# Softmax without the shift pass: exponentials straight from PSUM with row sums, in a three-stage token pipeline on one core

## The reference

```python
tokens = einsum('bpi,hi->bph', patches, W) + b            # embedding: 2352 -> 128, times pos_embed
# A: 8 heads of 16, complex q, k, v; scores * decay mask; group norm; silu gate; w2
# B: layer norm, then softmax attention over the 97 tokens, 8 heads of 16, scale 1/4
x2 = layernorm(h1);  q, k, v = x2 @ Wq + bq, x2 @ Wk + bk, x2 @ Wv + bv
p = softmax(q @ k.T / 4);  z = (p @ v) @ Wo + bo + x2
# C: layer norm, gate = softmax(th @ gate_W), the best expert of each token,
#    out = residual + gate weight * (gelu(th @ W1[e] + b1[e]) @ W2[e] + b2[e])
```

## Time and profile before

| | us |
|---|---|
| median of three timed runs | 1430.12 (1424.32 to 1433.03) |
| profiled execution, time | 1419.48 |
| profiled execution, span of its instructions | 1417.7 |
| TensorE busy | 1348.5 (95%) |
| VectorE busy | 1010.9 (71%) |
| ScalarE busy | 722.7 (51%) |
| GpSimd busy | 408.4 (29%) |

### The profile page before, as it was taken

The page is one execution under the profiler, slowest core; times in us unless marked ns, Lnnn a source line. Parts: engine busy times, 40 slices in busy tenths (PEclk is TensorE's granted clock), DMA queues, the critical chain, the costliest instruction groups (busy, mean ns, idle before and its releaser), DMA issues.

```text
span 1417.7 us, 40337 instructions
## 1 busy us (share of the span) xinstructions
PE 1348.5 (95%) x14878; PEld 989.9 (70%) x14879; DVE 1010.9 (71%) x2331; ACT 722.7 (51%) x1630; POOL 408.4 (29%) x268
## 2 busy tenths in 40 slices
PE   6889999999999999999999999999999775999996
PEld 5556666666666666666666666666666444999996
DVE  1477777777777777777777777777778853766664
ACT  2145555555555555555555555555555543556553
POOL 0000222222222222222222222222222233656664
PEclk9999999999999999999999999999999975999999
DMA  8522332232223322323232222222320011343331
GB/s 292 215 83 72 83 84 83 84 83 83 84 84 83 84 84 84 83 83 84 83 84 83 84 84 84 83 84 83 84 83 14 14 30 37 105 125 103 103 101 48
DMA packets 94842, 124.61 MB, mean 88 GB/s; under 512 B 56587, under 2 KB 77117, under 8 KB 94176
## 3 DMA queue, kind: packets, MB, share of 16 engines
q1 hardware_dynamic: 38112, 102.47, 23.1%
q0 software_dynamic: 56576, 19.93, 6.5%
HBM read 101.27 MB, written 20.82 MB: 86 GB/s over the span
## 4 chain that ended last, share of the span: by engine, by line
PE 90%; DVE 4%; DMA 2%; issue 2%; ACT 1%; POOL 0%; SPq 0%; POOLq 0%; DVEq 0%; ACTq 0%
PE bank_emb L421 20%; PE bank_s L475 9%; PE bank_z L411 7%; PE bank_y L489 7%; PE bank_x L411 7%; PE bank_s L710 6%; PE bank_s L553 4%; PE bank_s L541 4%; PE bank_s L411 3%; PE bank_y L411 3%; PE bank_y L581 3%; PE bank_x L699 3%; PE bank_y L699 3%; PE bank_x L563 3%; PE bank_s L525 2%; PE bank_y L553 2%
## 5 line engine op out<-in xcount | busy, mean ns | idle before, releaser
L1397 POOL DMA_INDIRECT expert_rows<-row_sb,placei x128 | 275.7, 2154 | 627.7 <-DVE z L1058 575.6
L421 PE MATMUL bank_emb<-home_x 128*128 128x256 f32 (+1 forms) x1216 | 324.0, 393 | 3.5 <-DMA home_x<-in_x_main 2.5
L421 PEld LDWEIGHTS bank_emb<-home_x 128*128 128x128 f32 (+1 forms) x1216 | 221.4, 192 | 103.4 <-issue 47.4
L998 DVE TENSOR_TENSOR home_s<-bank_s,con 97x776 f32<-97x776 f32 x256 | 239.8, 958 | 25.9 <-PE bank_s L475 13.8
L1012 DVE TENSOR_REDUCE mx<-bank_s 97x8 f32<-97x776 f32 x128 | 120.3, 960 | 57.9 <-PE bank_s L541 57.8
L1409 POOL DMA_INDIRECT out_tokens<-yo,tok x104 | 123.1, 1184 | 73.6 <-issue 52.5
L475 PE MATMUL bank_s<-qm,xn 32*97 32x452 f32 x1024 | 132.6, 580 | 4.2 <-DVE home_s L1017 2.0
L1017 DVE TENSOR_TENSOR home_s<-bank_s,mx 97x776 f32<-97x776 f32 x128 | 120.6, 963 | 3.3
L853 ACT ACTIVATE home_s<-home_s 97x776 f32<-97x776 f32 x128 | 108.4, 847 | 26.4 <-DVE home_s L1017 26.4
L710 PE MATMUL bank_s<-w2e,home_s 128*128 x832 | 110.6, 276 | 0.0
L1005 DVE COPY vp<-bank_s 97x128 f32<-97x128 f32 x256 | 70.1, 285 | 54.9 <-PE bank_s L475 54.8
(11 more groups left out here) (206 smaller groups left out, 2339.8 us busy)
## 6 DMA issues: line engine op xcount, KB each, us to landing
home_x<-in_x_main SPq DMA_DIRECT2D x96, 768.0 KB, 7.2
home_x<-expert_rows SPq DMA_DIRECT2D x104, 129.0 KB
w1e<-in_exp_w SPq DMA_DIRECT2D x1, 2576.0 KB, 10.8
txt<-in_txt_t SPq DMA_DIRECT2D x32, 64.0 KB, 2.3
w2e<-in_exp_w SPq DMA_DIRECT2D x1, 2048.0 KB, 16.1
expert_rows<-row_sb,placei POOLq DMA_INDIRECT x128, 8.1
out_tokens<-yo,tok POOLq DMA_INDIRECT x104
home_x<-in_x_tail SPq DMA_DIRECT2D x32, 48.0 KB, 2.6
```

The costliest lines, as they stand in the source:

```text
L421: mm = pe.matmul(banks["emb"][:, 0:NPG], wtok[0:k, c, :], x_sb[0:k, c, :], start=(c == 0), stop=(c == KC - 1))
L998: ins = dve.tensor_tensor(sm[:, k % 2, 2 * h:2 * h + 2, :], pair(h), decay, ALU.mult)
L1397: pool.indirect_dma_start(out=rows[:, :], out_offset=bass.IndirectOffsetOnAxis(ap=placei[:, k, c:c + 1], axis=0), in_=row_sb[:, k, c, E:E ...
```

## The change

- B's scores carry the opposite sign (bq4 and the scale of B.q are negative). VectorE takes the minimum of each block (b_min), and ScalarE computes exp(minimum - score), head by head and sequence by sequence, straight from the score banks: 32 ACTIVATEs of 97x97 a group with the minimum as bias column and with the row sum as second output into `rsum`. b_shift is gone; the banks are drained by the last exponential of each pair.
- The row sums come from there. VectorE makes their reciprocals, spread over 16 columns each (97x512 in one instruction, sums_reciprocal), TensorE transposes these (four 97x128 tiles, b_sums) and ScalarE copies the result to `rden` (sums_copy). The 16 matmuls, the logarithm and the exponential are gone.
- The lists of the three engines and the banks in `USES` are new. A group's a_center moves from the pass before into its own, b_q, b_scores of the first half and part of the copies move one pass later, c_rank and the placing too; the loop starts one pass later (FIRST = -1) and the first list is made one pass later. The embedding is cut in 11 pieces a pass.
- At the start, token weights and images come in turns and first, then columns and position, then weights and constants; TensorE does the whole embedding of group 0 before the products of the weights. ScalarE copies `woc` first. The blank rows are written behind the expert weights.
- rsb and rsc share a buffer with sqb and sqc.
- The block ends without GpSimd's drain.

```diff
-    block = ctx.enter_context(nc.Block())
+    block = ctx.enter_context(nc.Block(no_gpsimd_drain=True))
...
             def b_exp(g, k, h):
-                read(act, g, f"B.scores{k}.{h}")
-                p = prob[:, k, 2 * h:2 * h + 2, :].rearrange("p g t -> p (g t)")
-                act.activation(p, p, ACT.Exp).then_inc(s_prob, 1)
+                act.wait_ge(s_mx, MAXED[g, k, h])
+                if g:
+                    act.wait_ge(s_rden, g)
+                for r in (2 * h, 2 * h + 1):
+                    for j in range(4):
+                        t = slice(j * S, (j + 1) * S)
+                        ins = act.activation(prob[:, k, r, t], bank_s[0:S, r, t], ACT.Exp, scale=-1.0,
+                                             bias=mx[:, k, r, j:j + 1], accum_out=rsum[:, 2 * k + j // 2, r, j % 2:j % 2 + 1])
+                drain(ins, f"B.scores{k}.{h}")
...
-            def b_sums(g, k):
-                ps = use(g, "B.den") if k == 0 else banks[BANK_OF["B.den"]]
...
+            def b_sums(g):
+                pe.wait_ge(s_rden, g + 1)
+                ps = use(g, "B.den")
+                for c in range(G):
+                    mm = pe.transpose(ps[:, c * S:(c + 1) * S], rexp[:, c, :], const("ident")[0:S, 0:S])
+                done(mm, "B.den")
...
+            def sums_reciprocal(g):
+                for k in range(2):
+                    for h in range(2):
+                        read(dve, g, f"B.scores{k}.{h}")
+                dve.reciprocal(rexp[:].rearrange("p c (q d) -> p (c q) d", d=DH),
+                               rsum[:].rearrange("p c r o -> p (c r o)").unsqueeze(2).to_broadcast(
+                                   [S, G * H, DH])).then_inc(s_rden, 1)
...
+                at(b_q, i - 2)
+                at(a_gate, i - 1)
+                at(b_probs_t, i - 3, 1, 1)
+                at(b_sums, i - 3)
+                at(b_values, i - 3)
+                at(b_scores, i - 2, 0, first=True)
+                at(a_mix, i - 1, 0)
+                at(a_mix, i - 1, 1)
+                at(b_mix, i - 3, 0)
+                at(b_mix, i - 3, 1)
+                at(ahead, i, 16, 18)
+                at(c_rank, i - 4)
                 at(b_wo, i - 3)
+                at(ahead, i, 18, 19)
+                at(a_scores, i - 1, 2)
+                at(b_probs_t, i - 2, 0, 1)
+                at(ahead, i + 1, 0, 2)
                 at(c_var, i - 3)
+                at(ahead, i + 1, 2, 3)
+                at(a_center, i)
+                at(a_scores, i - 1, 3)
+                at(b_probs_t, i - 2, 0, 0)
+                at(ahead, i + 1, 3, 5)
+                at(a_var, i)
                 at(a_mix, i - 1, 2)
                 at(a_mix, i - 1, 3)
+                at(b_scores, i - 2, 1)
+                at(a_yvar, i - 1)
...
```

More of the change, by code:

```diff
@@ L225, in fusion @@
         sqc = sb("sqc", [P, N])
[L226 removed]
+        rsc = sqc
         th = sb("th", [P, N])
@@ L339, in _ @@
             for k in range(4):
+                if k < 3:
+                    sp.dma_start(wtok[:, XP[k]:XP[k + 1], :], w_main[:, XP[k]:XP[k + 1], :]).then_inc(s_w[k], 16)
+                else:
+                    sp.dma_start(wtok[0:KTAIL, KC - 1, :], w_tail).then_inc(s_w[k], 16)
                 load_x(0, k)
+            sp.dma_start(col[:], columns).then_inc(s_c, 16)
+            sp.dma_start(pos[:], pos_t).then_inc(s_c, 16)
+            sp.dma_start(wts[:], weights).then_inc(s_k, 16)
+            sp.dma_start(con[:], consts).then_inc(s_k, 16)
             def load_txt(i):
@@ L358, in _ @@
             sp.dma_start(w2e[:], exp_w2).then_inc(s_ew, 16)
+            sp.wait_ge(s_blankin, 16)
+            sp.dma_start(rows[E * REG:E * REG + P, :], blank[:]).then_inc(s_blankin, 16)
             with sp.Fori(2, NG) as i:
@@ L549, in b_probs_t @@
                 ps = use(g, name)
-                pe.wait_ge(s_prob, PROB[g, k, r // 2])
+                read(pe, g, f"B.scores{k}.{r // 2}")
                 for j in range(4):
@@ L554, in b_probs_t @@
                 done(mm, name)
-            def b_sums(g, k):
-                ps = use(g, "B.den") if k == 0 else banks[BANK_OF["B.den"]]
-                for r in range(4):
-                    read(pe, g, f"B.probs_t{k}.{r}")
-                for o in range(2):
-                    for r in range(4):
-                        src = pt[:, k, r, :].rearrange("p (c o t) -> p c o t", c=2, o=2)[:, :, o, :]
-                        mm = pe.matmul(ps[32 * r:32 * r + 32, 2 * k * S:(2 * k + 2) * S],
-                                       const("den", S)[:, 32 * o:32 * o + 32], src, start=(o == 0), stop=(o == 1),
-                                       skip_group_check=True)
-                if k == 1:
-                    done(mm, "B.den")
+            def b_sums(g):
[4 more added lines that the diff above has]
+                done(mm, "B.den")
             def b_mix(g, k):
@@ L686, in _ @@
+                at(b_probs_t, i - 2, 1, 3)
+                at(ahead, i + 1, 11, 12)
+                at(b_center, i - 1)
+                at(a_scores, i, 1, first=True)
+                at(b_var, i - 1)
+                at(ahead, i + 1, 12, 15)
+                at(b_probs_t, i - 2, 1, 0)
+                at(b_probs_t, i - 2, 1, 2)
+                at(a_scores, i, 0)
+                at(b_probs_t, i - 2, 0, 2)
+                at(b_k, i - 1)
+                at(ahead, i + 1, 15, 16)
                 if i == LISTED:
@@ L754, in _ @@
             act.wait_ge(s_mm, 1)
+            act.copy(woc[:], banks["s2"][:, 0:P]).then_inc(s_made, 1)
             act.copy(ar[:], banks["s0"][:, 0:P])
@@ L761, in _ @@
                              banks["s1"][r32, 0:2 * P].rearrange("p (m w) -> p m w", m=2)[:, :, r32])
-            act.copy(woc[:], banks["s2"][:, 0:P]).then_inc(s_made, 1)
             act.wait_ge(s_mm, 2)
@@ L842, in b_query @@
                 ps = full(act, g, "B.q")
-                drain(act.activation(q2[:], ps[:, 0:N], ACT.Identity, bias=bq4[:], scale=0.25), "B.q")
+                drain(act.activation(q2[:], ps[:, 0:N], ACT.Identity, bias=bq4[:], scale=-0.25), "B.q")
             def b_value_rows(g):
@@ L858, in b_probs_copy, with sums_copy @@
                 drain(act.copy(pt[:, k, r, :], ps[0:S, 0:4 * S]), name)
-            def sums_log(g):
+            def sums_copy(g):
                 ps = full(act, g, "B.den")
-                drain(act.activation(rden[:], ps[:, 0:N], ACT.Ln), "B.den")
-            def sums_reciprocal(g):
-                read(act, g, "B.den")
-                act.activation(rden[:], rden[:], ACT.Exp, scale=-1.0).then_inc(s_rden, 1)
+                drain(act.copy(rden[:], ps[:, 0:N]), "B.den")
             def free_rows(g):
@@ L1049, in b_divide @@
             def b_divide(g):
-                dve.wait_ge(s_rden, g + 1)
+                read(dve, g, "B.den")
                 ps = full(dve, g, "B.o")
@@ L1267, in _ @@
             for i in range(FIRST, LAST):
+                at(a_decayed, i - 1, 0, 0, last=True)
+                at(exp_sum, i - 4)
+                at(a_value_rows, i - 1, 0, 1)
+                at(a_decayed, i - 1, 0, 1, last=True)
+                at(b_key, i - 2, 0)
+                at(b_key, i - 2, 1, last=True)
+                at(gate_one, i - 1)
+                at(b_min, i - 2, 0, 0)
+                at(gate_times, i - 1)
+                at(gate_weight, i - 4)
+                at(b_min, i - 2, 0, 1)
```

259 lines of the change are left out of this document (108 added, 151 removed), and 20 rows, old and new, of the table USES.

## The result

The changed kernel takes 1484.75 us (median of 4 runs, 1482.79 to 1489.2) against 1429.55 (4 runs) before: a ratio of 1.039, 95% interval 1.035 to 1.043. The forecast was 1407 us, 1384 to 1442. The profiled execution took 1484.14 us, its span is 1482.3 us, 64.6 more than before.

What follows compares the result with a forecast made beforehand. Phase 1 was taken as bound by TensorE in the middle, load order at the start and the last group's chain; 3 + 6 + 7 + 7 = 23 us off 1419.5 gave 1396.5, as timed median 1407, range 1384 to 1442.

Steps and rivals of the forecast that it cites:

- The fixed parts: Outside the steady passes: start, tail of phase 1 and end together, forecast to bring 20 us.
- TensorE's own work: Steady pass on TensorE: 0.5 us less, 34.3 us a pass if nothing waits; bounds 33.9 and 34.8.
- waits for the score banks: TensorE waiting in each pass for banks held by ScalarE's exponentials: 0.4 us a pass at X = 0.33.
- The reciprocal: VectorE, end of the pass, 97x512: 0.65 us, up to 2.0, with 0.8 us of room, so no wait.
- Rival (e): VectorE's reciprocal takes 5.1 us, B's scores wait 3.6 us a pass behind B's keys, 1508 us; chance 0.04.
- X: Price of one 97-column ScalarE exponential with row sum: 0.33 us, 0.26 bare plus 0.07 readout; range 0.26 to 0.45.
- The first window: From B's first scores to A.scores2: 16 exponentials begin at 1.6, TensorE wants s2 at 6.6; room 5.0 us, X up to 0.31.
- The second window: From A.yvar to A.scores1: exponentials done at 4.0 + 16X, TensorE wants s0 at 9.1; room 5.1 us, X up to 0.32.
- rival (d): X = 0.45; TensorE waits 2.2 us at A.scores2 and 2.1 at A.scores1 every pass, 1515 us; chance 0.15.
- Start: Loads and first products: embedding 0 from 6, A.center 0 at 24.1, about 6 us gained; bounds 0 and 9.
- tail: Last groups of phase 1: shorter chain from A.center to C.rank, 7 us gained; bounds 0 and 20.
- end: Kernel's end without Pool's 10 us drain: 7 us less; lower bound 0 if the wait is only moved.

Runs made afterwards that it cites:

- sums_by_vector: Changed kernel without the exponentials' second output; VectorE adds the finished exponentials in four gaps, reciprocal narrow (97x32, then a copy): 1349.67 us, ratio 0.9515 to before.
- recip32: Changed kernel with the reciprocal taken of the 97x32 row sums, then spread to 97x512 by a VectorE copy: 1409.68 us, ratio 0.994 to before.
- recip32_window1: recip32 with A.scores2 cut in halves, a transpose of B and two embedding chunks between them: 1441.00 us, ratio 1.007 to before.
- recip32_window2: recip32 with one embedding chunk moved ahead of A.q_real and C.rows 0 and one ahead of A.scores1: 1419.50 us, ratio 0.995 to before.
- recip32_shift_embed: recip32_window2 with two chunks of the next embedding placed ahead of an undivided A.scores2: 1422.86 us, ratio 0.998 to before.
- reciprocal_moved: Changed kernel with the 97x512 reciprocal kept but moved ahead of the drains of A.scores1 on VectorE: 1489.02 us (one run).
- no_row_sum: Changed kernel with no second output of the exponentials, row sums set to 1 once, softmax not normalised: 1407.23 us, ratio 0.991 to before.
- recip32_no_row_sum: Changed kernel with the narrow reciprocal plus copy and no second output of the exponentials, normalisation left out: 1349.93 us (one run), ratio 0.951 to before.
- recip32_windows12: recip32_window1 plus one embedding chunk moved ahead of A.q_real and C.rows 0 and one ahead of A.scores1: 1429.44 us, ratio 1.000 to before.
- before_start: Kernel before with only the new order of loads and first products at the start: 1419.88 us, ratio 0.995 to before.
- before_both_ends: Kernel before with the new start and without GpSimd's drain at the end: 1414.19 us, ratio 0.992 to before.

## Why the prediction was wrong

The forecast was 1396.5 us on the profiled execution; it took 1484.1, 87.6 more. The fixed parts were 3 better than forecast, the pass was 37.73 instead of 34.7. By the steps of the prediction, measured from step to step in the usual pass of the changed kernel and of sums_by_vector (medians over 300 to 1000 us):

| term, us a pass | forecast | measured |
|---|---|---|
| TensorE's own work | 34.3 | 33.5 |
| waits for the score banks | 0.4 | 1.9 |
| wait for the reciprocal | 0 | 1.7 |
| stall for "issue" in A.mix | none | 0.6 |

The sum is 37.7, the usual pass 37.63 and the mean 37.73.

**The reciprocal, the step that failed.** The prediction bounded it by two rows and took 0.65, "the row it is nearest to in width". It is 3.353, above the upper bound of 2.0. Reading a price per element from 169 ns against 158 was the mistake: at 4 elements nearly all of either is the fixed part, so the 11 ns between them say nothing of the slope, and a bound derived from them is none. Nor is a shift's pace a likeness for another operation because it is as wide. With the rows at hand now, 97x4 0.17, 97x32 0.35, 97x512 3.353, the slope is 6.3 ns an element ((3353 - 170) / 508), against 1.24 for the shift (963 ns for 776), five times. The repeat count of 8 that the Trainium skill gives (VectorE: DVE Perf Modes, First, the fixed hardware budget) pointed the right way; eight shifts' time would be 5.1 us, and this trace shows 3.35.

**Rival (e)** thus told the mechanism, the place and the engine: 2.7 past the forecast less 0.8 of room would be 1.9 of wait, and 1.7 was measured. Its price was too high (3.6) and its chance of 0.04 too low for a cost that only a row of 4 elements spoke against. That the edit had no row of its width was a reason to give both ends weight.

**X, rightly priced.** 0.26 bare was 0.225 (16 in 3.82 us, of which the last takes 0.45), 0.07 for the readout 0.09, 0.33 together 0.318. Two errors in it offset each other. The 0.268 estimated from the Trainium skill (ScalarE: Activation LUTs, What ACT_TABLE_LOAD costs) was too long, as were the rows' 0.26.

**The windows, the second step that failed.** The price of the exponentials was right and the room for them was not. The first window was to cost 0.1 at this X (1.6 + 16 x 0.318 against 6.6), and it cost 1.0. Its exponentials begin 1.94 us after B's scores, not 1.6: the minimum begins 0.94 after them, where the forecast had 0.63 with a handover of 0.2, a term that no row stood behind. The last readout ends 0.2 later than sixteen times X (709.14 against 703.85 + 5.09). And TensorE asks for s2 at 6.3, not at 6.6: A.scores2 starts 6.25 after B's scores (701.91 to 708.16), and its third and fourth head don't come half of the run later, as the forecast had it. In sums_by_vector, where nothing waits, the first instructions of all four heads start within 0.02 us (702.40 to 702.42). Here the third head's stands at 709.19, 0.05 after the last readout has ended. These are 0.34, 0.20, 0.34 and 0.05 on top of the 0.1.

The second window was to cost nothing at this X and costs 0.9. Its exponentials are done 9.3 us after A.yvar starts (719.25), where the forecast's own sum gives 9.1. But TensorE asks for s0 at 8.6, not at 9.1 (711.84 to 720.40 in sums_by_vector). It pays in two places: 0.5 at C.rows 0, which needs a bank of the exponentials ahead of it and was overlooked, and 0.4 at A.scores1. These are the waits that rival (d) named, at nearly half its size and without its cause, an X of 0.45.

**TensorE's own work** was 0.8 too high, below the lower bound of 33.9. The transposes of the sums take 0.33, not 0.40: the forecast took a third of 1.19 us, the duration shown for twelve, and from start to start these are 1.03 (732.41 to 733.44). The charge for more cuts was wrong: a piece of one chunk takes 0.44 ahead of a product (734.67 to 735.11 in the changed kernel), the same as a chunk of a long piece; the 0.53 of the earlier trace rows is its price only ahead of B's scores. In all the embedding takes 8.6 us a pass and took 9.0 before, although it has two pieces more. And the eight transposes set apart cost 0.1 together, not 0.2.

**Start, tail, end.** Where the earlier trace rows had 16.57, embedding 0 began at 5.88 (forecast 6), and A.center 0 stood at 21.72 (28.87 before, forecast 24.1) with two more chunks done, 8.0 us gained instead of 6: the constants were there 0.7 earlier than foreseen (neg_wqi starts at 17.27), and from there to the end of the products it is 3.1 us, not 4.6. TensorE of the changed kernel at its start:

```profile
5.88 10.81 PE L428 MATMUL bank_emb<-home_x 128*128 128x256 f32 x38 [5.88 <-DMA home_x<-in_x_main]
...
21.72 0.81 PE L416 MATMUL bank_x<-h,con 128*128 128x388 f32 x2
```

The tail gave 10 (7), the end 6 (7). The drain of the earlier trace rows is absent, and its wait did not move to another place: the last scatter is issued at 1479.69, and the span ends at 1482.3. By their ratios the start and the drain are worth 0.5% and 0.7% in the kernel before, the size of the two terms; for the start the traces of that kernel leave it open, as said above.

**The chances.** The two causes are additive and of one size. With the reciprocal alone as forecast, recip32 is the whole change: 0.994, so 1421 us by the 1429.55 of before, within 1% of it and inside the range. That would have been luck in part: in recip32 the waits for the score banks are 1.4 us a pass above the forecast and TensorE's own work 0.8 below it. The side on which the time fell hung on the reciprocal.

## What to carry to other kernels

An operation that the trace doesn't show at its width is not priced by a row of a few elements: take it from a row of another shape only if two shapes give its slope, and otherwise make the small form (32 reciprocals, then a copy) from the start. A second output of an activation costs little by itself, but it lies on the way of whoever waits for the operand's bank; the same sum on an engine with gaps was free here. And for a window in which one engine must be done before another comes back, read both of its ends from the rows: when the first can begin (0.94 us after the scores here, not 0.63), and when the other really asks for the bank. Heads that run at the same time ask for all their banks at once.

## What the runs showed of the hardware

- A reciprocal on VectorE costs 6.3 ns an element of a row (97x512 in 3.353 us, 97x32 in 0.35, two of 97x16 in 0.36, 97x4 in 0.17), where the copy of 97x512 from the same kind of operand took 0.43 us.
- An activation's row sum is an instruction of its own behind it. It adds 0.09 us from start to start (0.318 against 0.225 for 97 columns).
- Small matmuls with 32 rows of weights each, for four heads on four banks, run at the same time: A.scores takes 0.95 us from step to step with all four heads and 0.93 with two (recip32_window1). Cut in two, the run takes 1.86.
- A wait inside a run of matmuls on several banks (A.scores2, 2.03 us instead of 1.01) is not in TensorE's own view of waits; it is in that of its weight loads (16 times, 0.8 us at most, for ScalarE's exponentials).
- In some kernels TensorE stops for 0.3 to 0.4 us inside the run of 64 small matmuls of A.mix, at the same place of nearly every pass, with nothing to wait for that the profile shows, and the pass is 0.6 longer. It is in the changed kernel, recip32_window2, recip32_shift_embed and reciprocal_moved, not in recip32, no_row_sum, recip32_no_row_sum and sums_by_vector. In recip32_window1 and recip32_windows12 the run is 0.2 longer, in before_start and before_both_ends one such run is 0.3 longer. Such stops in B.mix come in some passes of every kernel with the new lists. In the kernel before it comes with the new start and not with the drain left out; beyond that it follows neither an edit nor a wait, and what it is stays open.
